# Counting edges per node: POOL makes the higher digit of four tiles in sixteen

## The chip, the cores and the metric

The kernel runs on one core of one Trainium2 chip. The metric is device time in microseconds for one launch, median of several runs. Engines: PE is TensorE, DVE is VectorE, ACT is ScalarE, POOL is GpSimd, SP is the queue that issues transfers.

## The reference, cut to what matters

```python
s, t = src, dst                       # 412500 edges, 12500 nodes
qe = (q[s] * scale) + edge_attr @ q_rpe_w + q_rpe_b
ke = k[t] + edge_attr @ k_rpe_w + k_rpe_b
ve = v[t] + edge_attr @ v_rpe_w + v_rpe_b
compat = einsum('ehd,ehd->eh', qe, ke)
attn = exp(compat - segment_max(compat, s)[s]) / segment_sum(...)
out = segment_sum(ve * attn, s)
return layernorm(x + out)
```

The edges are sorted by `dst`, and the softmax and the sums are over `s`. The kernel therefore needs, for each of the 12500 source nodes, how many edges it has (`deg`) and where its run of records begins (`base`). The change is in the counting of these edges alone.

## The kernel before, in words

There are three stages, one after the other: `tables_stage` (counts the edges of each node and makes the tables of q, k and v), `sort_stage` (writes one record per edge to its node's place in DRAM) and `attend_stage` (softmax and sums). The change is in `tables_stage`, which lasts to about 419 us.

A node number is split into a lower digit (7 bits, 128 values) and a higher digit (98 values, `NB`). The edges stand in 3232 tiles of 128, one edge to a partition. For one tile TensorE multiplies a one-hot matrix of the lower digits (128x128) by a one-hot matrix of the higher ones (128x98) and adds the product to `ps_hist` in PSUM, which counts edges by both digits. Tiles are taken in 202 groups of 16 (`GT`), with two sets of buffers (`NG`). For a group:

- VectorE makes `h_lo` for all 16 tiles in one instruction (L280, 2048 elements per partition) and `h_hi` for the first ten in another (L282, 980 elements). Each compares two operands that lie in SBUF: the table `value` and the digits.
- ScalarE makes the higher digit of the last six (`SIGNS`) as the sign of (digit - column + 0.5) over 99 columns, one instruction a tile (L388), with an input in PSUM. The product with `h_lo` is added to `ps_sign`. The difference of neighbouring columns is twice a one-hot, and it is halved at the end (L317, L318).
- TensorE (`tally`) waits for `one_rows`, does ten products (L344), waits for `hi_signs`, does six more (L348) and raises `tallied`. For the first 98 groups a product of the table of q, k, v (L361) follows each tally.

`tallied` starts at two, so that VectorE and ScalarE may make group g once group g-2 is tallied. After its first 12 groups VectorE works on the destination's windows and digits (L291 to L302) before it goes on. SP issues the transfers in a fixed order, and those of `xt` that TensorE's later products need stand behind ones that wait for this work. POOL sets a few constants (L229 to L239) and then does nothing until the next stage; there it issues the scatter of the records.

Only the later stages show POOL at arithmetic: in `attend_stage` it multiplies a part of the values by the probabilities (L1176), and makes a mask in two steps, `beyond` (L898, a subtraction of two operands) and `past` (L902, a comparison with zero, then a multiplication), with a semaphore between them. VectorE's large instructions there (L1176, L996) read one operand from SBUF and one from PSUM.

Of the kernel before, what the change touches and what calls it, by code (L numbers as in the profile page):

```python
# [8 lines left out]
BF16 = mybir.dt.bfloat16  # L9
I16 = mybir.dt.int16  # L10
I32 = mybir.dt.int32
ALU = mybir.AluOpType
# [3 lines left out]
P = 128  # L16
# [4 lines left out]
NB = math.ceil(N / P)  # L21
# [30 lines left out]
def gnn_kernel(nc, x, xT, src_lin, src_tiles, dst_lin, dst_tiles, attr, qkv_w, qkv_b, k_rpe_w, k_rpe_b,  # L52
# [9 lines left out]
    with ExitStack() as keep:  # L62
        def kept(name, shape, dt=F32):
            return keep.enter_context(nc.sbuf_tensor(name, shape, dt))

        T = dict(
            iota_row=kept("iota_row", [P, P], BF16),
            iota_f=kept("iota_f", [P, P]),
            iota_p=kept("iota_p", [P, 1]),
            ident=kept("ident", [P, P]),  # L70
            later=kept("later", [P, P]),
            q_tab=kept("q_tab", [P, NB, DH]),
            base=kept("base", [P, NB]),
            deg=kept("deg", [P, NB]),
            w_attr=kept("w_attr", [P, FEAT]),

            y=kept("y", [P, NB, DIM]),
            more=kept("more", [1, NB], I32),
            win_row=kept("win_row", [1, NCH], I32),
            flag=kept("flag", [1, 1], I32),  # L80
        )
        digits = keep.enter_context(ExitStack())
        T["lo_f"] = digits.enter_context(nc.sbuf_tensor("lo_f", [P, NT], F32))
        T["hi_f"] = digits.enter_context(nc.sbuf_tensor("hi_f", [P, NT], F32))
        T["src_f"] = digits.enter_context(nc.sbuf_tensor("src_f", [P, NT], F32))
        tables_stage(nc, T, xT, src_lin, src_tiles, dst_lin, qkv_w, qkv_b, k_rpe_w, k_rpe_b,
                     q_rpe_w, q_rpe_b, v_rpe_w, v_rpe_b, lo_dram, src_dram, dl_dram, win_dram, over_dram, kv_dram,
                     rec_dram)
        sort_stage(nc, T, x, attr, dst_tiles, lo_dram, src_dram, dl_dram, kv_dram, rec_dram)
        digits.close()  # L90
        attend_stage(nc, T, rec_dram, out)


def tables_stage(nc, T, xT, src_lin, src_tiles, dst_lin, qkv_w, qkv_b, k_rpe_w, k_rpe_b,
# [3 lines left out]

    iota_row, iota_f, iota_p, ident, later = (T[k] for k in ("iota_row", "iota_f", "iota_p", "ident", "later"))
    lo_f, hi_f, src_f, q_tab = (T[k] for k in ("lo_f", "hi_f", "src_f", "q_tab"))
    base, deg, w_attr = (T[k] for k in ("base", "deg", "w_attr"))
    win_row, flag = T["win_row"], T["flag"]
    GT, PAIRS, NG = 16, 8, 2
    SIGNS = 6
    HPAIRS = (GT - SIGNS) // 2
    GROUPS = NT // GT
    NXG = NB // XG
    with ExitStack() as ctx:  # L110
        def sb(name, shape, dt=F32):
            return ctx.enter_context(nc.sbuf_tensor(name, shape, dt))

        def sem(name):
            return ctx.enter_context(nc.semaphore(name))
# [6 lines left out]
        hi_w = sb("hi_w", [P, NT], BF16)  # L122
# [14 lines left out]
        h_lo = [sb(f"h_lo{i}", [P, PAIRS, P, 2], BF16) for i in range(NG)]  # L137
        h_hi = [sb(f"h_hi{i}", [P, HPAIRS, NB, 2], BF16) for i in range(NG)]
        s_hi = [sb(f"s_hi{i}", [P, SIGNS, NB + 1], BF16) for i in range(NG)]
        cols_half = sb("cols_half", [P, NB + 1])  # L140
        signs = sb("signs", [P, NB + 1])
        zeros = sb("zeros", [P, P], BF16)
# [5 lines left out]
        ps_sign = ctx.enter_context(nc.psum_tensor("ps_sign", [P, 512], F32))  # L148
# [6 lines left out]
        iotas, consts, diag = sem("iotas"), sem("consts"), sem("diag")  # L155
# [4 lines left out]
        narrowed, widened = sem("narrowed"), sem("widened")  # L160
        one_rows, tallied = sem("one_rows"), sem("tallied")
        half_made, half_copied, hi_signs = sem("half_made"), sem("half_copied"), sem("hi_signs")
        sums_made, rows_summed = sem("sums_made"), sem("rows_summed")
        tail_zero, tail_out = sem("tail_zero"), sem("tail_out")
        x_in = [sem(f"x_in{i}") for i in range(2)]
# [61 lines left out]
        @block.gpsimd  # L227
        def _(pool):
            pool.iota(iota_i[:, :], pattern=[[1, P]], base=0, channel_multiplier=0).then_inc(iotas, 1)  # L229
            pool.iota(iota_pi[:, :], pattern=[[0, 1]], base=0, channel_multiplier=1).then_inc(iotas, 1)  # L230
            pool.memset(ident[:, :], 0.0).then_inc(diag, 1)
            pool.memset(later[:, :], 1.0).then_inc(diag, 1)
            pool.wait_ge(diag, 2)
            pool.affine_select(out=ident[:, :], in_=ident[:, :], compare_op=ALU.not_equal, fill=1.0,
                               base=0, pattern=[[-1, P]], channel_multiplier=1).then_inc(diag, 1)

            pool.affine_select(out=later[:, :], in_=later[:, :], compare_op=ALU.is_gt, fill=0.0,
                               base=0, pattern=[[1, P]], channel_multiplier=-1).then_inc(diag, 1)
            pool.memset(tail[:, :], 0.0).then_inc(tail_zero, 1)  # L239
            pool.wait_ge(diag, 4)  # L240

        @block.vector
        def _(dve):
# [30 lines left out]
            def one_hots(g, i):  # L274

                def tiles(t, pairs, n):
                    return t[:, bass.ds(GT * g, 2 * pairs)].rearrange("p (k a t) -> p k a t", a=1, t=2).broadcast_to((P, pairs, n, 2))
# [3 lines left out]
                                  ALU.is_equal)  # L281
                dve.tensor_tensor(h_hi[i][:, :, :, :], value[:, 0:NB, :].unsqueeze(1).broadcast_to((P, HPAIRS, NB, 2)), tiles(hi_w, HPAIRS, NB),  # L282
                                  ALU.is_equal).then_inc(one_rows, 1)
# [49 lines left out]
        @block.tensor  # L333
        def _(pe):
            pe.sem_inc(tallied, NG)
            pe.wait_ge(consts, 5)
            for ps in (ps_hist, ps_sign):
                nc.tensor.matmul(ps[:, 0:NB + 1], zeros[:, :], zeros[:, 0:NB + 1], start=True, stop=False,
                                 skip_group_check=True)

            def tally(g, i):
                pe.wait_ge(one_rows, g + 1)
                for k in range(GT - SIGNS):
                    nc.tensor.matmul(ps_hist[:, 0:NB], h_lo[i][:, k // 2, :, k % 2], h_hi[i][:, k // 2, :, k % 2],  # L344
                                     start=False, stop=False, skip_group_check=True)
                pe.wait_ge(hi_signs, g + 1)
                for k in range(GT - SIGNS, GT):
                    last = nc.tensor.matmul(ps_sign[:, 0:NB + 1], h_lo[i][:, k // 2, :, k % 2], s_hi[i][:, k - (GT - SIGNS), :],  # L348
                                            start=False, stop=False, skip_group_check=True)
                last.then_inc(tallied, 1)  # L350

            pe.wait_ge(wq_in, 32)
            with pe.Fori(0, NXG // 2) as it:
                for i in range(2):
                    for b in range(XG):
                        tally(2 * XG * it + XG * i + b, (XG * i + b) % NG)
                        if b == 0:
                            pe.wait_ge(x_in[i], 16 * it + 16)

                            pe.wait_ge(q_read, 2 * it + i + 1)  # L360
                        last = nc.tensor.matmul(ps_x[i][:, b, :], xt[i][:, b * P:(b + 1) * P], w_qkv[:, :],  # L361
                                                start=True, stop=True)
                    last.then_inc(x_done, 1)
            with pe.Fori(NB // NG, GROUPS // NG) as it:
                for i in range(NG):
                    tally(NG * it + i, i)
            pe.wait_ge(sums_made, 1)
            pe.wait_ge(diag, 4)
            nc.tensor.matmul(ps_row[:, 0:1], later[:, :], incl[:, NB - 1:NB], start=True,
                             stop=True).then_inc(rows_summed, 1)  # L370

        @block.scalar
        def _(act):
# [11 lines left out]
            def higher(g, i):  # L385
                act.wait_ge(tallied, g + 1)
                for k in range(SIGNS):
                    last = act.activation(s_hi[i][:, k, :], ps_half[:, 0:NB + 1], ACT.Sign, scale=-1.0,  # L388
# [828 lines left out]
```

## Time and profile before

| what | value |
|---|---|
| three runs | 6689.97, 6712.76 (median), 6715.67 us |
| the profiled execution's own time | 6723.71 us |
| its span | 6722.0 us |
| stage of the change | to about 419 us of the span |
| DVE, ACT, PE, POOL busy over the span | 69%, 46%, 54%, 53% |

The profiled execution took 11 us more than the median of the runs. Shares of busy time are means over three stages with different limits, so the stage of the change is to be read by itself. In the rows below, durations of a single instruction are ns in groups by form, and us in timelines; a timeline row is start, duration, engine, line, operation, tiles, shape, and in brackets the engine's idle time before it. Instructions of one engine overlap a little, so the distance between two starts can be less than the first one's duration.

### The profile page before, as it was taken

What the parts mean: (1) busy time and instruction counts of PE and PEld (TensorE: products, weight loads), DVE (VectorE), ACT (ScalarE), POOL (GpSimd) and SP (SyncE); (2) the same over time, 40 slices, a digit from 0 to 9 for tenths busy, and PEclk for the clock granted to TensorE, in tenths of its full rate; (3) what the DMA queues carried; (4) which work ended last, traced back from release to release, by engine and by line L of the source; (5) the groups of instructions that cost most, each with busy time, mean ns of one, the idle gap of its engine ahead of it and who ended that gap; (6) DMA issues with size and microseconds to landing.
All of it is one profiled execution on the core that took longest, in us unless ns stands there. A gap on an engine that the chain in (4) does not pass through costs nothing. (4 is left out here: it accounts for less than half of the span.)

```text
span 6722.0 us, 113212 instructions
## 1 busy us (share of the span) xinstructions
PE 3642.7 (54%) x22344; PEld 3336.9 (50%) x22344; DVE 4669.1 (69%) x18275; ACT 3058.9 (46%) x7584; POOL 3596.2 (53%) x4030
## 2 busy tenths in 40 slices
PE   4654555545545555554555555545455554386786
PEld 3544445444445444444445454445454444365665
DVE  7986666666666666666666666666666666598998
ACT  5964444444444444444444444444444444322332
POOL 0025555555555555555555555555555555565664
PEclk8976665666666666666666666666666666698999
DMA  2013333333333333333333333333333333497897
GB/s 74 19 48 93 95 94 95 98 95 96 97 96 95 97 96 95 94 97 95 98 96 96 94 96 97 93 95 98 92 96 95 96 96 94 133 374 305 339 367 269
DMA packets 628039, 821.65 MB, mean 122 GB/s; under 512 B 216092, under 2 KB 561885, under 8 KB 615007
## 3 DMA queue, kind: packets, MB, share of 16 engines
q1 hardware_dynamic: 510185, 373.02, 21.9%
q0 software_dynamic: 117824, 448.32, 18.1%
q14 instruction: 22, 0.18, 0.0%
q8 instruction: 8, 0.13, 0.0%
HBM read 644.87 MB, written 176.01 MB: 122 GB/s over the span
## 5 line engine op out<-in xcount | busy, mean ns | idle before, releaser
L542 POOL DMA_INDIRECT rec_dram<-recs,place_i x3232 | 3093.7, 957 | 2751.9 <-DVE recs L596 1828.1
L630 PE MATMUL ps_cnt<-hi_hot,lo_hot 128*128 128x98 bf16 x3232 | 371.1, 259 | 2563.8 <-ACT free_rec L691 1615.5
L674 ACT ACTIVATE lo_hotT<-lo_b,minus_p 128x512 f32<-128x512 bf16 x808 | 582.9, 721 | 2585.8 <-DMA w_in<-kv_dram 2300.2
L573 DVE SCALAR_TENSOR_TENSOR matches<-src_b,src_f,ps_const 128x128 bf16<-128x128 int16 (+3 forms) x3232 | 1582.3, 543 | 67.7 <-issue 52.5
L630 PEld LDWEIGHTS ps_cnt<-hi_hot,lo_hot 128*128 128x128 bf16 x3232 | 239.0, 120 | 2730.4 <-issue 2420.5
L639 PE MATMUL ps_look<-free_rec,lo_hotT 128*128 128x98 f32 x6464 | 1408.2, 389 | 2.9 <-ACT lo_hotT L680 2.9
L656 PE MATMUL ps_feat<-w_in,edge_in 115*128 115x128 f32 x6464 | 1348.3, 375 | 44.8 <-issue 44.5
L582 DVE CUSTOM_DVE_ANT_0 picked<-hi_hot,ps_look 128x98 f32<-128x98 bf16 x3232 | 642.3, 252 | 1015.2 <-remote 803.0
L639 PEld LDWEIGHTS ps_look<-free_rec,lo_hotT 128*128 128x128 f32 x6464 | 1286.1, 294 | 3.1 <-ACT lo_hotT L680 3.1
L656 PEld LDWEIGHTS ps_feat<-w_in,edge_in 115*128 115x128 f32 x6464 | 1247.9, 286 | 43.6 <-issue 43.4
L962 PE MATMUL ps_sum<-msg,ident 128*128 128x256 f32 x2744 | 624.5, 386 | 237.7 <-DVE msg L1176 237.7
L596 DVE TENSOR_REDUCE recs<-qk 128x16 f32<-128x128 f32 x808 | 231.3, 286 | 661.5 <-remote 537.4
L962 PEld LDWEIGHTS ps_sum<-msg,ident 128*128 128x128 f32 x2744 | 518.6, 192 | 343.3 <-DVE msg L1176 275.2
L680 ACT ACTIVATE lo_hotT<-lo_hotT,one 128x512 f32<-128x512 f32 x808 | 573.3, 710 | 0.0
L683 ACT ACTIVATE edge_in<-edge_in,one 96x512 f32<-96x512 f32 x808 | 573.1, 709 | 0.0
L676 ACT ACTIVATE edge_in<-dst_b,minus_p 96x512 f32<-96x512 bf16 x808 | 570.0, 705 | 0.0
L564 DVE TENSOR_TENSOR lo_hot<-lo_f,ps_const 128x512 bf16<-128x512 bf16 (+1 forms) x808 | 551.7, 683 | 12.6 <-issue 12.6
L566 DVE TENSOR_TENSOR hi_hot<-hi_f,ps_const 128x392 bf16<-128x392 bf16 (+1 forms) x808 | 449.2, 556 | 8.1 <-issue 7.8
L667 ACT ACTIVATE recs<-ps_feat 128x384 f32<-128x384 f32 x808 | 379.9, 470 | 2.8 <-DMA rec_dram<-recs,place_i 1.7
L1121 ACT ACTIVATE ps_prob<-ps_lg,neg 128x56 f32<-128x56 f32 x392 | 109.3, 279 | 536.1 <-DVE neg L1011 536.1
L388 ACT ACTIVATE s_hi<-ps_half,hi_f 128x99 bf16<-128x99 f32 x1212 | 303.5, 366 | 77.7 <-PE ps_sign L348 77.4
L691 ACT ACTIVATE free_rec<-ps_cnt 128x98 f32<-128x98 f32 x808 | 188.3, 233 | 330.7 <-remote 305.5
(152 smaller groups left out, 3419.1 us busy)
## 6 DMA issues: line engine op xcount, KB each, us to landing
lo_b<-lo_dram SPq DMA_DIRECT2D x808, 128.0 KB
src_b<-src_dram SPq DMA_DIRECT2D x808, 128.0 KB
dst_b<-dl_dram SPq DMA_DIRECT2D x808, 96.0 KB
rec_dram<-recs,place_i POOLq DMA_INDIRECT x3232
edge_in<-in_attr SPq DMA_DIRECT2D x808, 36.0 KB
w_in<-kv_dram SPq DMA_DIRECT2D x808, 36.0 KB
kv_dram<-kvt SPq DMA_DIRECT2D x14, 336.0 KB, 2.7
xt<-in_xT SPq DMA_DIRECT2D x14, 224.0 KB, 3.3
```

What stands on the lines that cost most here:

```text
L542: pool.indirect_dma_start(rec_dram[:, :], bass.IndirectOffsetOnAxis(place_i[j][:, m:m + 1], 0), recs[j][:, m, :], None).then_inc(scattered ...
L564: dve.tensor_tensor(lo_hot[j][:, :, :], lo_f[:, tiles].unsqueeze(2).broadcast_to((P, CT, P)), ps_const[:, 0:1, :].broadcast_to((P, CT, P)) ...
L573: last = dve.scalar_tensor_tensor(matches[j][:, m, 0:before], src_b[j][:, 0:before], src_f[:, bass.ds(u * CT + m, 1)], ps_const[:, CT - m: ...
L582: ins = dve.tensor_tensor_reduce(out=picked[j][:, m, :], in0=hi_hot[j][:, m, :], in1=ps_look[j % 2][:, m, 0:NB], scale=1.0, scalar=0.0, op ...
L630: last = nc.tensor.matmul(ps_cnt[:, 0:NB], lo_hot[j][:, m, :], hi_hot[j][:, m, :], start=False, stop=False, skip_group_check=True)
L639: last = nc.tensor.matmul(ps_look[j % 2][:, m, 0:NB], lo_hotT[j][:, P * m:P * (m + 1)], free_rec[j % 2][:, :], start=True, stop=True)
L656: last = nc.tensor.matmul(ps_feat[j][:, m, :], edge_in[j][0:K_ROWS, tile], w_in[j][0:K_ROWS, :], start=True, stop=True)
L674: act.activation(lo_hotT[j][:, :], lo_b[j][:, :], ACT.Abs, bias=minus_p[:, 0:1]).then_inc(lo_off, 1)
L676: act.activation(edge_in[j][0:WIN, :], dst_b[j][:, :], ACT.Abs, bias=minus_p[0:WIN, 0:1]).then_inc(dst_off, 1)
L680: act.activation(lo_hotT[j][:, :], lo_hotT[j][:, :], ACT.Relu, scale=-1.0, bias=one[:, 0:1]).then_inc(lo_hotT_made, 1)
L683: act.activation(edge_in[j][0:WIN, :], edge_in[j][0:WIN, :], ACT.Relu, scale=-1.0, bias=one[0:WIN, 0:1]).then_inc(dst_hotT_made, 1)
L962: last = nc.tensor.matmul(ps_sum[i][:, 0:SUM, :], ident[:, :], msg[i][:, k:k + SUM, :], start=(k == 0), stop=(k + SUM == S0))
```

## The change

The first ten tiles of a group are divided anew. VectorE makes one-hots of the higher digit for six (`HPAIRS` goes from 5 to 3). For the next four (`STEPS`) POOL makes steps: it subtracts the column number from the digit (`fall`, 4x99 elements per partition, two operands in SBUF, bf16), waits for that, and turns the difference into 2 where it is at least zero and 0 elsewhere (`t_hi`). The difference of neighbouring columns of such a step is twice a one-hot, as with the signs, so TensorE adds the products with these tiles to `ps_sign`. It waits for `hi_steps` before them. POOL waits for `tallied` like the other two.

```diff
--- before.py
+++ after.py
@@ -98,13 +98,14 @@
 
 
 
+
     iota_row, iota_f, iota_p, ident, later = (T[k] for k in ("iota_row", "iota_f", "iota_p", "ident", "later"))
     lo_f, hi_f, src_f, q_tab = (T[k] for k in ("lo_f", "hi_f", "src_f", "q_tab"))
     base, deg, w_attr = (T[k] for k in ("base", "deg", "w_attr"))
     win_row, flag = T["win_row"], T["flag"]
     GT, PAIRS, NG = 16, 8, 2
-    SIGNS = 6
-    HPAIRS = (GT - SIGNS) // 2
+    SIGNS, STEPS = 6, 4
+    HPAIRS = (GT - SIGNS - STEPS) // 2
     GROUPS = NT // GT
     NXG = NB // XG
     with ExitStack() as ctx:
@@ -137,6 +138,8 @@
         h_lo = [sb(f"h_lo{i}", [P, PAIRS, P, 2], BF16) for i in range(NG)]
         h_hi = [sb(f"h_hi{i}", [P, HPAIRS, NB, 2], BF16) for i in range(NG)]
         s_hi = [sb(f"s_hi{i}", [P, SIGNS, NB + 1], BF16) for i in range(NG)]
+        t_hi = [sb(f"t_hi{i}", [P, STEPS, NB + 1], BF16) for i in range(NG)]
+        fall = [sb(f"fall{i}", [P, STEPS, NB + 1], BF16) for i in range(NG)]
         cols_half = sb("cols_half", [P, NB + 1])
         signs = sb("signs", [P, NB + 1])
         zeros = sb("zeros", [P, P], BF16)
@@ -160,6 +163,7 @@
         narrowed, widened = sem("narrowed"), sem("widened")
         one_rows, tallied = sem("one_rows"), sem("tallied")
         half_made, half_copied, hi_signs = sem("half_made"), sem("half_copied"), sem("hi_signs")
+        hi_falls, hi_steps, pool_groups = sem("hi_falls"), sem("hi_steps"), sem("pool_groups")
         sums_made, rows_summed = sem("sums_made"), sem("rows_summed")
         tail_zero, tail_out = sem("tail_zero"), sem("tail_out")
         x_in = [sem(f"x_in{i}") for i in range(2)]
@@ -238,6 +242,22 @@
                                base=0, pattern=[[1, P]], channel_multiplier=-1).then_inc(diag, 1)
             pool.memset(tail[:, :], 0.0).then_inc(tail_zero, 1)
             pool.wait_ge(diag, 4)
+            pool.wait_ge(consts, 5)
+            pool.wait_ge(narrowed, 2)
+
+            def higher(g, i):
+
+                pool.wait_ge(tallied, g + 1)
+                pool.sem_inc(pool_groups, 1)
+                pool.tensor_tensor(fall[i][:, :, :], hi_w[:, bass.ds(GT * g + 2 * HPAIRS, STEPS)].unsqueeze(2).broadcast_to((P, STEPS, NB + 1)),
+                                   iota_row[:, 0:NB + 1].unsqueeze(1).broadcast_to((P, STEPS, NB + 1)), ALU.subtract).then_inc(hi_falls, 1)
+                pool.wait_ge(hi_falls, g + 1)
+                pool.sem_inc(pool_groups, 1)
+                pool.tensor_scalar(t_hi[i][:, :, :], fall[i][:, :, :], 0.0, 2.0, ALU.is_ge, ALU.mult).then_inc(hi_steps, 1)
+
+            with pool.Fori(0, GROUPS // NG) as it:
+                for i in range(NG):
+                    higher(NG * it + i, i)
 
         @block.vector
         def _(dve):
@@ -340,8 +360,12 @@
 
             def tally(g, i):
                 pe.wait_ge(one_rows, g + 1)
-                for k in range(GT - SIGNS):
+                for k in range(2 * HPAIRS):
                     nc.tensor.matmul(ps_hist[:, 0:NB], h_lo[i][:, k // 2, :, k % 2], h_hi[i][:, k // 2, :, k % 2],
+                                     start=False, stop=False, skip_group_check=True)
+                pe.wait_ge(hi_steps, g + 1)
+                for k in range(STEPS):
+                    nc.tensor.matmul(ps_sign[:, 0:NB + 1], h_lo[i][:, HPAIRS + k // 2, :, k % 2], t_hi[i][:, k, :],
                                      start=False, stop=False, skip_group_check=True)
                 pe.wait_ge(hi_signs, g + 1)
                 for k in range(GT - SIGNS, GT):
```

## Rows read from the trace of the kernel before

**Rows 1.** The page of the profile: busy share in 40 slices

```profile
DVE  7986666666666666666666666666666666598998
```

**Rows 2.** Busy time by stretch (x is instructions; then clock, DMA)

```profile
300.00:400.00 100.00, 53.43 (x930) 44.65 (x931) 100.00 (x118) 88.17 (x352) 0.00 (x0) 1.00 0.00 0
```

**Rows 3.** Groups of instructions by form, 80 to 400 us

```profile
L388 ACT ACTIVATE s_hi<-ps_half,hi_f 128x99 bf16<-128x99 f32 x1066 | 267.2, 365 | 56.0 <-PE ps_sign L348 55.8
L280 DVE TENSOR_TENSOR h_lo<-value,lo_w 128x2048 bf16<-128x2048 bf16 x178 | 216.1, 1214 | 27.7 <-PE ps_sign L348 27.6
L282 DVE TENSOR_TENSOR h_hi<-value,hi_w 128x980 bf16<-128x980 bf16 x177 | 116.6, 659 | 0.0
```

**Rows 4.** The timeline of one beat, 299 to 304 us

```profile
300.35 1.21 DVE L280 TENSOR_TENSOR h_lo<-value,lo_w 128x2048 bf16<-128x2048 bf16 x1
...
300.49 0.64 PE L344 MATMUL ps_hist<-h_hi,h_lo 128*128 128x98 bf16 x10 [0.79 <-DVE h_hi L282]
...
301.56 1.51 ACT L388 ACTIVATE s_hi<-ps_half,hi_f 128x99 bf16<-128x99 f32 x6 [0.21 <-PE ps_sign L348]
302.06 1.21 DVE L280 TENSOR_TENSOR h_lo<-value,lo_w 128x2048 bf16<-128x2048 bf16 x1
```

**Rows 5.** POOL's instructions by form, whole span

```profile
L1176 POOL TENSOR_TENSOR msg<-rec,prob_s 128x1024 f32<-128x1024 f32 x98 | 198.0, 2021 | 47.1 <-ACT prob_s L1132 47.1
...
L905 POOL TENSOR_TENSOR known<-rec,past 128x224 f32<-128x224 f32 x98 | 58.0, 592 | 41.0 <-DMA rec<-rec_dram,idx 34.5 <-POOL past L902 4.9
L902 POOL TENSOR_SCALAR past<-beyond 128x56 f32<-128x56 f32 x98 | 40.4, 412 | 19.3 <-POOL beyond L898 19.3
...
L898 POOL TENSOR_TENSOR beyond<-iota_f,deg 128x56 f32<-128x56 f32 x98 | 27.4, 280 | 0.0
L887 POOL COPY idx<-start_i 128x1 int32 x92 | 16.7, 181 | 44.2 <-DVE msg L1176 43.7
...
L234 POOL TENSOR_SCALAR_AFFINE_SELECT ident<-ident 128x128 f32<-128x128 f32 x1 | 0.3, 293 | 0.2 <-POOL later L232 0.2
```

**Rows 6.** The timeline, 6201 to 6219 us: VectorE and POOL together

```profile
6199.51 2.02 POOL L1176 TENSOR_TENSOR msg<-rec,prob_s 128x1024 f32<-128x1024 f32 x1 [0.45 <-ACT prob_s L1132]
6200.11 1.45 DVE L1049 TENSOR_SCALAR past_x<-iota_f,left 128x16 f32<-128x16 f32 x1
...
6201.48 0.29 POOL L898 TENSOR_TENSOR beyond<-iota_f,deg 128x56 f32<-128x56 f32 x1
6201.60 0.15 DVE L1050 TENSOR_SCALAR next_x<-next_x  x1
...
6201.97 0.41 POOL L902 TENSOR_SCALAR past<-beyond 128x56 f32<-128x56 f32 x1 [0.20 <-POOL beyond L898]
```

**Rows 7.** Line 1176: count, then duration in ns, least, median, most

```profile
L1176 DVE TENSOR_TENSOR msg<-rec,ps_prob x196: 1454/1478/1489, 5879.5 to 6684.9; 128x1280 f32<-128x1280 f32 x196
L1176 POOL TENSOR_TENSOR msg<-rec,prob_s x98: 2009/2021/2030, 5878.2 to 6683.5; 128x1024 f32<-128x1024 f32 x98
```

**Rows 8.** The timeline, 6000 to 6025 us: two large products side by side

```profile
6004.60 2.02 POOL L1176 TENSOR_TENSOR msg<-rec,prob_s 128x1024 f32<-128x1024 f32 x1 [0.37 <-ACT prob_s L1132]
...
6004.95 1.48 DVE L1176 TENSOR_TENSOR msg<-rec,ps_prob 128x1280 f32<-128x1280 f32 x1
```

**Rows 9.** The timeline, first 46 us: VectorE waits, and turns to the windows

```profile
24.22 1.23 DVE L280 TENSOR_TENSOR h_lo<-value,lo_w 128x2048 bf16<-128x2048 bf16 x1 [2.98 <-PE ps_sign L348]
...
41.70 4.41 DVE L291 TENSOR_REDUCE win_f<-dst_l 101x8 f32<-101x4096 int32 x1
```

**Rows 10.** The timeline, 59 to 100 us: VectorE comes back; a stall

```profile
59.51 1.22 DVE L280 TENSOR_TENSOR h_lo<-value,lo_w 128x2048 bf16<-128x2048 bf16 x1
...
61.37 1.00 PE L344 MATMUL ps_hist<-h_hi,h_lo 128*128 128x98 bf16 x10 [18.32 <-DVE h_hi L282]
...
93.73 0.79 PE L361 MATMUL ps_x<-w_qkv,xt 65*128 65x128 f32 x2 [27.48 <-DMA xt<-in_xT]
...
95.99 1.22 DVE L280 TENSOR_TENSOR h_lo<-value,lo_w 128x2048 bf16<-128x2048 bf16 x1 [27.58 <-PE ps_sign L348]
```

## The prediction

> **What bounds the kernel now.** I read the page first, for where the changed stage lies: VectorE is busy for 70 and 90% of the first two slices of 40, 168 us each, and for 60% or so in the long stage behind them [rows 1]. Then the busy time by stretch: between 300 and 400 us VectorE is busy for 100.00 us of 100, ScalarE for 88, TensorE for 53, POOL for 0, at the full clock (2.4 GHz) [rows 2]. So here VectorE sets the pace, ScalarE is close behind, and POOL is free. Then the groups by form, for the price of each part [rows 3], and the timeline, for the beat: one group begins at 300.35 us and the next at 302.06, so a group costs 1.71 us, though the durations add up to 1.214 + 0.659 = 1.87 [rows 3, 4]; an instruction starts before the one ahead has ended. ScalarE's six signs take 1.51 us and then it waits 0.21 for the tally, and TensorE waits 0.79 us for h_hi before each tally [rows 4]. The 202 groups cost 202 x 1.71 = 345 us. This stage comes before the others and none of it overlaps them, so what a group gains or loses is multiplied by 202 and reaches the end.
>
> **VectorE: what goes.** h_lo stays whole. h_hi shrinks from 980 to 588 elements. The two forms differ by 2048 - 980 = 1068 elements and 1214 - 659 = 555 ns, that is 0.52 ns an element [rows 3]; 392 elements fewer save 0.20 us. VectorE's own beat becomes 1.71 - 0.20 = 1.51 us. If nothing else were late, ScalarE at 1.51 us would be level with it and the stage would win 202 x 0.20 = 40 us. That is the most that the change can bring.
>
> **POOL: what is added.** Each group gets two instructions of 4 x 99 = 396 elements, the second waiting for the first.
> - The subtraction has two inputs in SBUF. POOL's such forms: 56 elements 280 ns, 224 elements 592, 1024 elements 2021 [rows 5]. The last two give 1429 / 800 = 1.79 ns an element, the first two 1.86. So 592 + 172 x 1.79 = 900 ns. These rows are float32; the new form is bf16, with one operand spread over 99 columns, which no row has. I take 0.90 us, with 0.80 to 1.10 as bounds.
> - Between two dependent instructions POOL sits idle for 0.20 us, as at 6201.97 us [rows 6].
> - The comparison and multiplication has one row, 56 elements for 412 ns [rows 5]. Its price per element is bounded below by the one-input rows, 1 element 181 ns and 128 elements 293 (0.88 ns an element), and above by the two-input slope. So 412 + 340 x 0.88 = 711 ns, or 412 + 340 x 1.79 = 1020 ns. I take the middle, 0.87 us: one input speaks for the low end, two operations for the high one.
>
> Alone, POOL needs 0.90 + 0.20 + 0.87 = 1.97 us for a group (bounds 1.71 to 2.32). That is more than the 1.71 us of now. Two sets of buffers don't help a stage whose throughput is too low: POOL becomes the pace even undisturbed.
>
> **Do the two engines disturb each other?** The trace has a place that shows that they can. At 6200.11 us VectorE starts an instruction on 16 elements, while POOL's multiplication runs from 6199.51 to 6201.53; VectorE's ends at 6201.56, after 1.45 us, and right behind it an instruction of the same kind on one element takes 0.15 us [rows 6]. The small one waited for POOL's to end, 0.03 us before. Not every pair does that: the one-element instruction ran beside POOL's `beyond` [rows 6], and VectorE's large products, of which one starts at 6004.95 us inside POOL's of 6004.60, take 1454 to 1489 ns in all 196 cases and POOL's 2009 to 2030 [rows 7, 8]. Those have one operand in PSUM, as the names ps_prob say. The new pairs are of neither kind: h_lo and h_hi read both operands from SBUF, and so does POOL's subtraction. No row has such a pair, so the price of standing together lies between nothing and the whole of both. I take the whole: the row that was blocked has all its operands in SBUF on both sides, as the new pairs have, and the large rows that were not blocked differ from them just by the PSUM operand. Then the instructions of the two engines take turns. POOL's 0.20 us of idling is covered by VectorE's turn, and a group costs 1.51 + 0.90 + 0.87 = 3.28 us. For its own range: 1.51 + 0.80 + 0.71 = 3.02 at the low end; if VectorE's instructions no longer start before the one ahead has ended, 1.87 - 0.20 + 1.10 + 1.02 = 3.79 at the high one.
>
> On this the Trainium skill has a rule (SBUF — State Buffer, section "Who interferes with whom"): a VectorE instruction with two SBUF inputs and a GpSimd instruction that reads SBUF share a read interface, whoever is first holds it for the whole instruction, and the other blocks; with at most one SBUF input and outside the two-port modes there is no conflict. The blocked row at 6200.11 and the undisturbed L1176 rows agree with it, but the rule's case for two SBUF inputs is shown by no row here. By the rule a group would cost what the turns above cost; with it wrong for tensor_tensor, the 1.97 us of POOL alone.
>
> **What is taken off again.** (a) At 24.22 us VectorE has waited 2.98 us for ScalarE's first signs [rows 9]; a slower start covers those 3 us. (b) From 41.70 to 59.51 us VectorE works on the windows [rows 9, 10], and in that time the steps of the two groups ahead are made with no VectorE instruction of the count beside them: 2 x 1.77 = 3.5 us. (c) After it TensorE stands 27.48 us for xt, which lands 34 us after VectorE came back [rows 10]; SP issues it behind transfers that wait for VectorE's window work, so it moves with that and not with the groups. The three groups tallied in those 34 us can each be 1.57 us slower for nothing: 5 us. Together 12 us.
>
> **What hangs on the new wait.** TensorE waits for `hi_steps` in the middle of a tally. Behind it stand four step products, six sign products and, in the first 98 groups, the product for the tables, for which ScalarE and then SP wait; all of them have a beat to spare. With TensorE idle for most of the beat its clock may fall to 1.2 GHz, where ten products take 1.00 us [rows 10] in place of 0.64 [rows 4]. The ten that follow POOL are late by that, but VectorE and POOL still have the other buffer's group before them, which takes longer. I cost it at nothing; without that cover it is 0.4 us a group. POOL's start is no cost: the digits that it waits for are those that VectorE's first h_hi needs. After its last group POOL goes on to the next stage, where it has nothing to send until later.
>
> **The sum.** 202 x (3.28 - 1.71) = 317 us, less 12, is +305 us. Against the profiled execution's own 6723.7 us that is 7029; this execution was 11 us over the median of the runs, so the median should come to about 7018. I say 7020. The range of this case: 202 x (3.02 - 1.71) - 12 = +253 to 202 x (3.79 - 1.71) - 12 = +408, that is 6965 to 7120.
>
> **The rivals.**
> - *No blocking, POOL is the pace.* For it: the large products keep their time side by side, and a one-element instruction too [rows 6 to 8]. Against: the blocked one [rows 6]. The price is 202 x (1.97 - 1.71) = +53 us; (a) and (c) take off 3 + 1 us, so 6713 + 49 = 6762. With POOL at its bounds, 1.71 to 2.32 us, it is 6709 to 6832.
> - *POOL is quick enough, and the change gains.* The other side: the one mechanism is that POOL's pair costs less than 1.71 us, with no blocking. For it only the low bounds above, both at once, and a smaller price for bf16, which no row shows. At 1.51 us ScalarE and VectorE set the pace: 6713 - 40 = 6673. It decides at 1.71 us for the pair.
> - *Blocking only for one of POOL's two instructions.* The second reads one operand in place of two; were it free of the turns, a group would cost VectorE's 1.51 plus the 0.90 us, 2.41 us, which also holds the pair with its wait: 202 x 0.70 - 8 = +133, 6846.
> - That the change doesn't do what it says can be ruled out: digit minus column is at least zero up to the digit's own column, so neighbouring columns of the steps differ by 2 there and by 0 elsewhere, which is what halving after the sums needs.
>
> **How the numbers follow.** Turns for both instructions 0.65, for one of them 0.08, no blocking with POOL as the pace 0.20, a gain or a draw 0.07. The predicted time is that of the first, 7020. The range has to take in most of the second and third, and the first one's bounds: 6735 to 7130, which leaves out the gain, the lower part of the third case and a little above. A measurement of this kernel can tell about 0.5%, 34 us, from no change. Of the third case about a fifth lies within that, and of the last about half gains more. So: faster 0.03, same 0.08, slower 0.89.
>
> **What would show it.** Right: VectorE and POOL alternate in the timeline between 100 and 700 us, the beat is 3.0 to 3.8 us, durations of h_lo or of POOL's pair are stretched over their price when they meet, h_hi alone is 0.45 us, and the count ends near 725 us in place of 419. The stages after it last as long as before. Wrong: h_lo at 1.21 us right beside a POOL instruction in progress (then the beat is POOL's 1.8 to 2.3 us); or POOL idle in each beat with TensorE waiting for ScalarE, which would be the gain.

## The result, and the profile after

The changed kernel takes 6994.05 us (median of 4 runs, 6980.8 to 7016.14) against 6711.2 us (4 runs) before: ratio 1.0431, 95% interval 1.0396 to 1.0466. It is 283 us slower (4.3%). The forecast was 7020 us.

The stage of the count is where the time went. Its first step after the counting is a copy of the sums to `signs`; here it is before and after, in the timelines (start, duration):

```profile
416.43 0.26 DVE L316 COPY signs<-ps_sign 128x99 f32<-128x99 f32 x1 [1.59 <-PE ps_sign L348]
```

```profile
701.00 0.26 DVE L336 COPY signs<-ps_sign 128x99 f32<-128x99 f32 x1 [4.37 <-PE ps_sign L372]
```

The count ends 284.6 us later. The spans of the two profiled executions differ by 269 us, so the later stages account for no loss.

The busy time by stretch of the changed kernel (PE, PEld, DVE, ACT, POOL, granted clock, share of transfers, GB/s), to be read against [rows 2]:

```profile
300.00:400.00 100.00, 59.71 (x549) 51.69 (x550) 57.02 (x63) 50.29 (x194) 93.95 (x64) 0.50 0.07 18
```

POOL is busy for 94 us of 100 and VectorE for 57 in place of 100. The granted clock is 0.50, TensorE's lower level of 1.2 GHz, where it was 1.00 before. The waits name the same pace (120 to 600 us; total, times, longest):

```profile
ACT s_hi L412 <- PE ps_sign L372: 242.8, 150, 2.3
...
PE ps_sign L368 <- POOL t_hi L256: 209.7, 150, 2.3
DVE h_lo L300 <- PE ps_sign L372: 204.4, 151, 1.9
```

In each group everyone waits for POOL's second instruction: TensorE directly, ScalarE and VectorE by way of the tally. POOL itself waits for nobody in this stretch; its only idle time is the 0.20 us between its two instructions. The groups by form, beside [rows 3]:

```profile
L256 POOL TENSOR_SCALAR t_hi<-fall 128x396 bf16<-128x396 bf16 x151 | 306.2, 2028 | 29.5 <-POOL fall L252 29.5
...
L300 DVE TENSOR_TENSOR h_lo<-value,lo_w 128x2048 bf16<-128x2048 bf16 x151 | 197.5, 1308 | 204.4 <-PE ps_sign L372 204.4
L252 POOL TENSOR_TENSOR fall<-hi_w,iota_row 128x396 bf16<-128x396 bf16 x150 | 150.7, 1005 | 0.0
...
L302 DVE TENSOR_TENSOR h_hi<-value,hi_w 128x588 bf16<-128x588 bf16 x151 | 92.7, 614 | 0.0
```

The means hide two kinds of group. The timeline, beside [rows 4], shows a pattern that repeats every two groups (TensorE left out but for one row):

```profile
639.82 0.85 POOL L252 TENSOR_TENSOR fall<-hi_w,iota_row 128x396 bf16<-128x396 bf16 x1
...
640.87 1.54 POOL L256 TENSOR_SCALAR t_hi<-fall 128x396 bf16<-128x396 bf16 x1 [0.20 <-POOL fall L252]
641.07 1.39 DVE L300 TENSOR_TENSOR h_lo<-value,lo_w 128x2048 bf16<-128x2048 bf16 x1 [1.93 <-PE ps_sign L372]
...
642.38 1.16 POOL L252 TENSOR_TENSOR fall<-hi_w,iota_row 128x396 bf16<-128x396 bf16 x1
642.38 0.45 DVE L302 TENSOR_TENSOR h_hi<-value,hi_w 128x588 bf16<-128x588 bf16 x1
...
642.46 0.52 PE L368 MATMUL ps_sign<-t_hi,h_lo 128*128 128x99 bf16 x4 [1.05 <-POOL t_hi L256]
...
643.62 1.23 DVE L300 TENSOR_TENSOR h_lo<-value,lo_w 128x2048 bf16<-128x2048 bf16 x1 [0.79 <-PE ps_sign L372]
...
643.74 2.51 POOL L256 TENSOR_SCALAR t_hi<-fall 128x396 bf16<-128x396 bf16 x1 [0.20 <-POOL fall L252]
644.77 0.77 DVE L302 TENSOR_TENSOR h_hi<-value,hi_w 128x588 bf16<-128x588 bf16 x1
646.22 0.85 POOL L252 TENSOR_TENSOR fall<-hi_w,iota_row 128x396 bf16<-128x396 bf16 x1
...
647.26 1.54 POOL L256 TENSOR_SCALAR t_hi<-fall 128x396 bf16<-128x396 bf16 x1 [0.20 <-POOL fall L252]
```

From 639.82 to 646.22 us two groups are made: 6.40 us, so a group costs 3.20 us where the forecast had 3.28. In the first, the comparison begins 0.20 us ahead of h_lo and takes 1.54 us; h_lo takes 1.39 in place of 1.21. In the second, h_lo begins 0.12 us ahead and the comparison takes 2.51 us. The subtraction takes 0.85 us by itself and 1.16 when h_hi starts with it.

### The profile page after: what moved, and what is told of

It is laid out like the page before. It is cut to its first block and busy times, and to the rows that moved or that the text cites. A ratio compares the mean times of both kernels' runs of the same rounds, so it can differ in the third digit from the quotient of the medians.

```text
span 6991.0 us, 114627 instructions
## 1 busy us (share of the span) xinstructions
PE 3741.4 (54%) x22344; PEld 3424.0 (49%) x22344; DVE 4693.4 (67%) x18275; ACT 3059.9 (44%) x7584; POOL 4203.3 (60%) x4434
## 5 line engine op out<-in xcount | busy, mean ns | idle before, releaser
L663 PE MATMUL ps_look<-free_rec,lo_hotT 128*128 128x98 f32 x6464 | 1386.5, 384 | 2.7 <-ACT lo_hotT L704 2.7
L680 PE MATMUL ps_feat<-w_in,edge_in 115*128 115x128 f32 x6464 | 1333.5, 372 | 46.7 <-issue 46.4
L663 PEld LDWEIGHTS ps_look<-free_rec,lo_hotT 128*128 128x128 f32 x6464 | 1265.8, 290 | 2.9 <-ACT lo_hotT L704 2.9
L300 DVE TENSOR_TENSOR h_lo<-value,lo_w 128x2048 bf16<-128x2048 bf16 x202 | 265.1, 1312 | 286.2 <-PE ps_sign L372 286.2
L256 POOL TENSOR_SCALAR t_hi<-fall 128x396 bf16<-128x396 bf16 x202 | 405.5, 2007 | 39.4 <-POOL fall L252 39.4
```

Source lines behind the costliest of these rows:

```text
L663: last = nc.tensor.matmul(ps_look[j % 2][:, m, 0:NB], lo_hotT[j][:, P * m:P * (m + 1)], free_rec[j % 2][:, :], start=True, stop=True)
L680: last = nc.tensor.matmul(ps_feat[j][:, m, :], edge_in[j][0:K_ROWS, tile], w_in[j][0:K_ROWS, :], start=True, stop=True)
```

## The experiments

In the expectations F is POOL's first instruction, the subtraction, and T its second, the comparison with its multiplication. A beat is the time from one group to the next. A hold is the time for which one engine keeps the other waiting.

**First set.** Here the kernel before took 6724.72 us (7 runs). Two of the four kernels (the first and the second) are the count's stage alone, with wrong counts; only where their count ends is of use. The time of the third is that of one run. The first takes POOL's reading away.

```diff
-                pool.tensor_tensor(fall[i][:, :, :], hi_w[...], iota_row[...], ALU.subtract).then_inc(hi_falls, 1)
-                pool.wait_ge(hi_falls, g + 1)
-                pool.tensor_scalar(t_hi[i][:, :, :], fall[i][:, :, :], 0.0, 2.0, ALU.is_ge, ALU.mult).then_inc(hi_steps, 1)
+                pool.memset(t_hi[i][:, :, :], 2.0).then_inc(hi_steps, 1)
```

> The stage of the count alone (the two later stages are left out, and POOL's two instructions are replaced by one that only fills t_hi with a constant, so the counts are not counts). Theory: POOL's own price (1.54 us for the comparison, 0.85 us for the subtraction) and the waits of the two engines for each other's SBUF operands are all of the loss, and the rest of the change is a gain. Then a group costs 1.51 to 1.55 us, ScalarE and VectorE set the pace, and the stage ends near 419 - 202 x 0.18 = 383 us. Rival: the split of the tally, with its wait in the middle and its slow-clock products, costs by itself: a group stays over 1.71 us and the stage ends at 419 us or later.

The timeline of this kernel near 300 us:

```profile
299.69 0.43 POOL L264 MEMSET t_hi<- 128x396 bf16 x1 [1.09 <-PE ps_sign L380]
300.00 1.21 DVE L308 TENSOR_TENSOR h_lo<-value,lo_w 128x2048 bf16<-128x2048 bf16 x1
...
301.13 0.45 DVE L310 TENSOR_TENSOR h_hi<-value,hi_w 128x588 bf16<-128x588 bf16 x1
301.20 0.43 POOL L264 MEMSET t_hi<- 128x396 bf16 x1 [1.08 <-PE ps_sign L380]
301.51 1.21 DVE L308 TENSOR_TENSOR h_lo<-value,lo_w 128x2048 bf16<-128x2048 bf16 x1
```

A beat is 1.51 us, h_lo takes 1.21 and h_hi 0.45 us with POOL's instruction beside them, and the copy to `signs` comes at 377.8 us, 38.6 us earlier than before. The split of the tally costs nothing here, and a POOL instruction that only writes disturbs nobody. The rest of the change is worth what the forecast had as its most, 40 us. One thing differs from the changed kernel besides POOL's reading: TensorE's granted clock was 1.00 between 200 and 300 us, against 0.50 there.

The second takes VectorE away: its one-hots are filled once ahead, and a fill of 96 elements (0.10 us) stands for them in the loop.

```diff
-                dve.tensor_tensor(h_lo[i][:, :, :, :], value[...], tiles(lo_w, PAIRS, P), ALU.is_equal)
-                dve.tensor_tensor(h_hi[i][:, :, :, :], value[...], tiles(hi_w, HPAIRS, NB), ALU.is_equal).then_inc(one_rows, 1)
+                dve.memset(h_hi[i][:, :, 0:16, :], 0.0).then_inc(one_rows, 1)
```

> The stage of the count alone, with VectorE's h_lo and h_hi made once ahead and only a 96-element fill in their place in the loop (two later stages and the true counts left out). Theory: POOL is the pace even undisturbed: F 0.85 us, 0.20 idle, T 1.54 us, a group every 2.56 us, and the wait for VectorE's reads goes from 0.64 us a group to nothing; no T of 2.51 us, no F of 1.16 us. The stage ends near 17 + 202 x 2.56 + 13 for the windows + about 20 for the transfer = 567 us. Rival: the 1.54 us of T are themselves waiting for VectorE, and POOL alone takes about 0.9 + 0.2 + 0.9 = 2.0 us a group: the stage ends near 450 us.

Its POOL instructions over all 202 groups (count, then duration in ns, least, median, most):

```profile
L264 POOL TENSOR_TENSOR fall<-hi_w,iota_row x202: 848/851/2047, 17.7 to 572.2; 128x396 bf16<-128x396 bf16 x101
L268 POOL TENSOR_SCALAR t_hi<-fall x202: 1538/1540/1547, 19.9 to 573.2; 128x396 bf16<-128x396 bf16 x101
```

A comparison never takes more than 1547 ns and never less than 1538: this is POOL's price and no wait. A group costs 2.56 us (comparisons begin at 299.64 and 302.20 us), and the copy comes at 575.9 us (567 expected), 159.5 us later than before. VectorE's part, put back, brings it to 701.0: another 125 us, or 0.62 us a group.

The third puts POOL's loop of the changed kernel (its function `higher` with both instructions) into the kernel before; VectorE, ScalarE and TensorE stay as they were, and none of them waits for it.

```diff
+            with pool.Fori(0, GROUPS // NG) as it:
+                for i in range(NG):
+                    higher(NG * it + i, i)
```

> The kernel before, whole and with right results, with POOL's two instructions run beside VectorE's full ones; nobody waits for them within the count, though the stage can't close before POOL is through. Asked: by how much VectorE's beat of 1.71 us grows. Theory of reads: POOL holds VectorE off only while it reads, about 0.65 us for the subtraction and 0.3 us for the comparison, in each of its own groups of 3 to 4 us: VectorE's beat is 2.1 to 2.3 us, and h_lo shows durations between 1.2 and 1.9 us. Theory of whole turns (the forecast's): VectorE's h_lo and h_hi and POOL's two take turns, the beat is about 1.71 + 0.85 + 1.54 = 4.1 us. Third: only POOL is held off, the beat stays 1.71 us.

Seven microseconds of it, VectorE and POOL:

```profile
297.93 1.73 POOL L256 TENSOR_SCALAR t_hi<-fall 128x396 bf16<-128x396 bf16 x1 [0.20 <-POOL fall L252]
298.18 1.53 DVE L300 TENSOR_TENSOR h_lo<-value,lo_w 128x2048 bf16<-128x2048 bf16 x1
...
299.63 1.36 POOL L252 TENSOR_TENSOR fall<-hi_w,iota_row 128x396 bf16<-128x396 bf16 x1
299.63 0.65 DVE L302 TENSOR_TENSOR h_hi<-value,hi_w 128x980 bf16<-128x980 bf16 x1
...
300.21 1.86 DVE L300 TENSOR_TENSOR h_lo<-value,lo_w 128x2048 bf16<-128x2048 bf16 x1
...
301.19 2.28 POOL L256 TENSOR_SCALAR t_hi<-fall 128x396 bf16<-128x396 bf16 x1 [0.20 <-POOL fall L252]
...
302.00 0.97 DVE L302 TENSOR_TENSOR h_hi<-value,hi_w 128x980 bf16<-128x980 bf16 x1
302.89 1.21 DVE L300 TENSOR_TENSOR h_lo<-value,lo_w 128x2048 bf16<-128x2048 bf16 x1
...
303.45 1.36 POOL L252 TENSOR_TENSOR fall<-hi_w,iota_row 128x396 bf16<-128x396 bf16 x1
...
304.03 1.31 DVE L302 TENSOR_TENSOR h_hi<-value,hi_w 128x980 bf16<-128x980 bf16 x1
...
305.26 1.53 DVE L300 TENSOR_TENSOR h_lo<-value,lo_w 128x2048 bf16<-128x2048 bf16 x1
```

From 298.18 to 305.26 us VectorE makes three groups, 2.36 us each, and POOL makes two (comparisons at 297.93 and 301.19, subtractions at 299.63 and 303.45). The amounts by which VectorE's instructions are stretched come in two sizes. A comparison of POOL's costs 0.32 us: h_lo 1.53 in place of 1.21, h_hi 0.97 in place of 0.65. A subtraction costs 0.65 us: h_lo 1.86, h_hi 1.31. Two of each in three groups are 1.94 / 3 = 0.65 us, and 1.71 + 0.65 is the beat of 2.36. Neither whole turns (4.1 us) nor an undisturbed VectorE (1.71 us) is left; the theory of reads holds, a little above its 2.1 to 2.3. Over the whole count the copy to `signs` comes at 543.9 us, 127.5 us later than before, or 0.63 us a group. The total of 6991.76 us means only that the stage can't close before POOL is through.

The fourth drops the second operation of the comparison.

```diff
-                pool.tensor_scalar(t_hi[i][:, :, :], fall[i][:, :, :], 0.0, 2.0, ALU.is_ge, ALU.mult).then_inc(hi_steps, 1)
+                pool.tensor_scalar(t_hi[i][:, :, :], fall[i][:, :, :], 0.0, None, ALU.is_ge).then_inc(hi_steps, 1)
-                    nc.tensor.matmul(ps_sign[:, 0:NB + 1], h_lo[...], t_hi[i][:, k, :], ...)
+                    nc.tensor.matmul(ps_sign[:, P:P + NB + 1], h_lo[...], t_hi[i][:, k, :], ...)
+            step(dve.scalar_tensor_tensor(signs[:, :], ps_sign[:, P:P + NB + 1], 2.0, signs[:, :], ALU.mult, ALU.add))
```

> The change, with right results, where POOL's second instruction compares but does not multiply (steps of 1, summed in columns of their own and doubled at the end, one instruction more on VectorE there). Theory A, the second operation is what made T cost 1.54 us: T falls to about 1.0 us, a group from 3.20 to 2.7 us, and the kernel takes about 6890 us. Theory B, the price is that of bf16 or of the elements and not of the second operation: T stays at 1.4 to 1.55 us and the kernel at 6980 to 7000 us.

```profile
298.67 1.13 POOL L252 TENSOR_TENSOR fall<-hi_w,iota_row 128x396 bf16<-128x396 bf16 x1
...
299.02 1.10 DVE L302 TENSOR_TENSOR h_hi<-value,hi_w 128x588 bf16<-128x588 bf16 x1
...
299.99 1.20 POOL L256 TENSOR_SCALAR t_hi<-fall 128x396 bf16<-128x396 bf16 x1 [0.20 <-POOL fall L252]
300.04 1.54 DVE L300 TENSOR_TENSOR h_lo<-value,lo_w 128x2048 bf16<-128x2048 bf16 x1
...
301.16 1.14 POOL L252 TENSOR_TENSOR fall<-hi_w,iota_row 128x396 bf16<-128x396 bf16 x1
...
301.51 1.11 DVE L302 TENSOR_TENSOR h_hi<-value,hi_w 128x588 bf16<-128x588 bf16 x1
...
302.49 1.20 POOL L256 TENSOR_SCALAR t_hi<-fall 128x396 bf16<-128x396 bf16 x1 [0.20 <-POOL fall L252]
```

6859.03 us, ratio to before 1.0203 (1.0177 to 1.0230). The comparison takes 1.20 us, so the second operation costs 0.34 us, not the 0.5 that theory A had; but the count ends at 567.4 us, 133.6 earlier than in the changed kernel, more than theory A's 100. The beat falls from 3.20 to 2.49 us, by twice what POOL saves, and the order in which the engines meet is another: POOL's comparison now begins just ahead of h_lo, group after group, and is not stretched (1197 ns at the least and in the median of all 202). That this order is what the rest of the gain comes from is read from the timeline, not tested by itself. Here VectorE is busy for 100.00 us of 100 and sets the pace: 1.51 us of its own, 0.33 for the comparison (h_lo 1.54) and 0.65 for the subtraction (h_hi 1.11) are 2.49.

**Second set.** This chip ran the kernel before in 5405.76 us (11 runs), so only differences are read; the count itself ends where it did (700.7 us in the second kernel below, against 701.0). The first makes steps for two tiles.

```diff
-    SIGNS, STEPS = 6, 4
+    SIGNS, STEPS = 6, 2
```

> The change for two tiles in sixteen in place of four (VectorE makes eight; right results). Theory of holds, from the runs so far: POOL keeps VectorE off while it reads, 0.65 us for the subtraction and 0.33 us for the comparison of four tiles, so about half for two; VectorE's beat is 1.61 + 0.33 + 0.17 = 2.1 us, VectorE is busy 100%, and POOL's pair alone (0.50 + 0.20 + about 0.9 = 1.6 us) is not the pace. Kernel: 6720 + 202 x 0.4 - 10 = 6790 us. Rival, POOL's price alone: the pair at 1.6 us is under 1.71 us, so the change gains, 6700 us. Rival, whole turns: 1.61 + 0.5 + 0.9 = 3.0 us, 6970 us.

5478.4 us (4 runs), 72.6 more than before (70 expected), ratio 1.0135 (1.0121 to 1.0150). The beat is 2.08 us (h_lo starts at 299.15 and 301.23 us): 1.61 us of VectorE's own, 0.15 us held by the comparison (h_lo 1.36 us) and 0.32 by the subtraction (h_hi 0.88), half of those for four tiles.

The second changes the type of the difference.

```diff
-        fall = [sb(f"fall{i}", [P, STEPS, NB + 1], BF16) for i in range(NG)]
+        fall = [sb(f"fall{i}", [P, STEPS, NB + 1]) for i in range(NG)]
```

> The change with the difference between POOL's two instructions in float32 (right results). Asked: is it bf16 that made the comparison cost 1.54 us where the float32 row of the kernel before gave 0.7 to 1.0? Theory A, no: price by element and operation; T undisturbed stays at 1.5 us and the kernel at about 6990 us. Theory B, the narrow type is slow to read: T undisturbed falls to about 1.0 us and the kernel to about 6880 us. A float32 operand is twice the bytes, so T may also hold VectorE for longer than 0.33 us.

5684.88 us (one run), 279 more than before, as with bf16 (283). The comparison takes 1537 ns at the least and 1538 in the median. The type is not it: theory A. Its price by size: 56 elements 412 ns [rows 5], 198 elements 892 ns (the least in the version for two tiles), 396 elements 1540 ns, so 3.3 ns an element with two operations.

The third and fourth have no subtraction. For four tiles, and then for two:

```diff
-                pool.tensor_tensor(fall[i][:, :, :], ...)
-                pool.tensor_scalar(t_hi[i][:, :, :], fall[i][:, :, :], 0.0, 2.0, ALU.is_ge, ALU.mult).then_inc(hi_steps, 1)
+                for k in range(STEPS):
+                    last = pool.tensor_scalar(t_hi[i][:, k, :], iota_row[:, 0:NB + 1], hi_f[:, tile:tile + 1], 2.0, ALU.is_le, ALU.mult)
+                last.then_inc(hi_steps, 1)
```

> The change for four tiles with no subtraction: one instruction a tile compares the 99 columns with the digit of each partition and doubles, so POOL reads one operand and not two (right results; POOL's loop is written out). Theory of holds: no hold of 0.65 us; four short ones, together 0.33 to 0.5 us, so VectorE could keep 1.51 + 0.4 = 1.9 us; POOL needs 4 x 0.55 = 2.2 us by the two rows of 56 and 396 elements (412 and 1540 ns), plus what it waits for VectorE, so POOL is the pace at 2.3 to 2.9 us: 6830 to 6940 us. Rival: what counts is how many instructions POOL starts while VectorE reads, each waiting for the end of VectorE's; then four a group cost more than two, 3.2 us or more, 7000 us.

> As the version with one instruction a tile, for two tiles (VectorE makes eight of the ten; right results). POOL's 2 x 0.55 = 1.1 us are far from the pace, so this is the gentlest form. Theory of holds: VectorE is let off 0.10 us a group and held for 0.17 to 0.3 us, since POOL's reading (0.33 us for 396 elements, 0.83 ns each) costs VectorE more than VectorE's own work on the element (0.52 ns): beat 1.68 to 1.85 us, the kernel 0 to 30 us slower than before, no gain. Rival: the holds vanish where POOL reads little at a time; beat 1.61 us, 20 us faster than before.

Groups by form of the two-tile version (120 to 360 us), of POOL and of VectorE:

```profile
L253 POOL TENSOR_SCALAR t_hi<-iota_row,hi_f 128x99 bf16<-128x99 bf16 x196 | 242.7, 1260 | 0.0
```

```profile
L298 DVE TENSOR_TENSOR h_lo<-value,lo_w 128x2048 bf16<-128x2048 bf16 x98 | 121.1, 1236 | 76.0 <-PE ps_sign L370 75.9
L300 DVE TENSOR_TENSOR h_hi<-value,hi_w 128x784 bf16<-128x784 bf16 x97 | 54.1, 558 | 0.0
```

Both expectations by holds failed, and on the same side. Four tiles: 5743.52 us, +338, ratio 1.0626 (1.0611 to 1.0642), worse than the change. Two tiles: 5547.86 us, +142, ratio 1.0263 (1.0249 to 1.0276), worse than with the pair, and outside the rival's too, which had a gain. VectorE is hardly held (h_lo 1236 ns, h_hi 558), but POOL is, and it became the pace: it is busy for 100.00 us of 100. The mean of 1260 ns hides two kinds again. Here are two instructions of POOL's in a row in the two-tile version:

```profile
300.85 0.64 POOL L253 TENSOR_SCALAR t_hi<-iota_row,hi_f 128x99 bf16<-128x99 bf16 x1
301.46 1.97 POOL L253 TENSOR_SCALAR t_hi<-iota_row,hi_f 128x99 bf16<-128x99 bf16 x1
```

The first meets no instruction of VectorE's. The second starts 0.15 us behind an h_lo (301.31 us) and lasts past the h_hi behind it (302.45 to 303.01 us), 1.33 us longer than its price. Of 404 instructions 198 are of this kind. With four tiles it is one in four (198 of 808 take over 1.5 us, and the median is 638 ns). So the rival for four tiles came near in time (it had 7000 us, +280 over its base), but not each instruction waits: one a group does.

**Last run.** VectorE's table goes to PSUM, for h_lo as shown and for h_hi alike. This kernel and the one before ran once each here.

```diff
+            step(dve.tensor_copy(ps_row[:, P:3 * P], value[:, :, :].rearrange("p n t -> p (n t)")))
+            value_p = ps_row[:, P:3 * P].rearrange("p (n t) -> p n t", t=2)
-                dve.tensor_tensor(h_lo[i][:, :, :, :], value[:, :, :]..., tiles(lo_w, PAIRS, P), ALU.is_equal)
+                dve.tensor_tensor(h_lo[i][:, :, :, :], value_p..., tiles(lo_w, PAIRS, P), ALU.is_equal)
```

> The change, with right results, where the table of digit values that VectorE compares with lies in PSUM, in float32, so h_lo and h_hi read one operand from SBUF and not two. VectorE's own work gets slower: about 1.2 to 1.3 ns an element by the row lo_hot of the kernel before (512 elements 683 ns), so h_lo 2.2 to 2.6 us and h_hi 0.7 to 0.8 us. Theory, the hold is for the second SBUF operand: POOL's pair is undisturbed in every group (the subtraction 0.85 us, the comparison 1.54 us, none of 1.16 or 2.51) and VectorE's h_lo and h_hi have one duration each (spread under 0.05 us); the beat is VectorE's own 2.9 to 3.3 us. Rival, any two instructions of the two engines that use SBUF wait for each other: durations spread by 0.3 to 1 us as in the changed kernel, and the beat is 3.5 us or more.

```profile
L302 DVE TENSOR_TENSOR h_lo<-ps_row,lo_w x202: 2268/2271/2292, 17.7 to 637.6; 128x2048 bf16<-128x2048 f32 x101
```

```profile
L304 DVE TENSOR_TENSOR h_hi<-ps_row,hi_w x202: 748/749/760, 19.9 to 639.8; 128x588 bf16<-128x588 f32 x101
```

```profile
L252 POOL TENSOR_TENSOR fall<-hi_w,iota_row x202: 848/848/2036, 16.5 to 635.3; 128x396 bf16<-128x396 bf16 x101
L256 POOL TENSOR_SCALAR t_hi<-fall x202: 1537/1538/1544, 18.7 to 636.4; 128x396 bf16<-128x396 bf16 x101
```

All four have one duration (the one subtraction of 2036 ns is the first, beside a cast of VectorE's), though both engines work at once: in 200 to 300 us VectorE is busy for 100.00 us and POOL for 82.93. The beat is VectorE's 2.88 us, and the kernel takes 5624.46 us against 5401.35, 223 more. So it is not enough that both engines use SBUF: with one operand of VectorE's in PSUM, neither holds the other off. The edit changes more than the operand's place, though. The table is float32, and h_lo takes 1.11 ns an element where the write-only version has 0.59. No run has a float32 table in SBUF, so that the place alone does it is likely and not shown.

## Why the prediction was right, and where its sum was not

*VectorE's part.* h_hi at 0.45 us and a beat of 1.51 us without POOL's reading: as forecast, shown by the write-only version.

*The subtraction.* 0.85 us against 0.90 forecast.

*The comparison.* 1.54 us against 0.87, beyond the bound of 1.02. The step of the sum that failed is the price per element, bounded by two inputs at 1.79 ns: a comparison and a multiplication of one input cost 3.3 ns an element. The middle was taken between bounds of which neither came from an instruction with two operations. The one row of the same form had a single size, and so no slope.

*Whole turns.* The forecast let VectorE's 1.51 us and POOL's pair exclude each other. In fact POOL holds VectorE off for 0.65 us of its subtraction's 0.85, but only for 0.33 us of its comparison's 1.54; and VectorE, if it reads first, holds POOL off to its end. Per two groups POOL loses 0.97 us at a comparison and 0.31 at a subtraction, 0.64 a group, where the forecast charged 1.51. So a group is 0.85 + 0.20 + 1.54 - 0.03 + 0.64 = 3.20 us against 0.90 + 0.87 + 1.51 = 3.28. Off by +0.67 for the comparison, -0.87 for the turns, +0.17 for an idle gap that nothing covers and -0.05 for the subtraction, the terms meet in nearly the same sum. The total was right by more luck than its steps deserve; that POOL becomes the pace, that both engines hold each other off, and the sign, were right for their reasons.

On the turns, the Trainium skill (SBUF — State Buffer, section "Who interferes with whom") has a VectorE instruction with two SBUF inputs against a GpSimd instruction that reads SBUF as a case that conflicts, and at most one SBUF input, or a GpSimd instruction that only writes, as cases that don't. The last run and the write-only one agree (h_lo 2268 to 2292 ns, 1203 to 1227 ns). It calls the shared ports an exclusive lock, and has whoever issues first keep them for the whole instruction; that sentence stands with VectorE's two-port modes, and the forecast carried it over to these reads. VectorE's h_lo does so here, but a comparison of 1.54 us kept h_lo off for 0.33 us.

*What was taken off.* 202 x (3.20 - 1.71) = 301 us, and the count ended 284.6 later: 16 us taken off, 12 forecast. TensorE's lower clock kept nobody waiting by itself: at 642.46 us the products of the steps start 0.05 us after the comparison ends (640.87 + 1.54), so none of the six products before them was in the way, and from 120 to 600 us POOL never waits for the tally. But h_lo starts when the tally ends, 1.16 us after those products begin, and by 0.12 or 0.20 us that decides which engine reads first. Products at the upper clock would end the tally sooner; no run has the changed kernel so, and what order and what beat would follow is open.

*The rivals.* POOL's price without any blocking (+49 us) fell short on both counts: alone it costs 159.5 us, and the blocking 125. The gain exists, 38.6 us, but only if POOL doesn't read. Blocking for one of POOL's instructions (6846 us) fell short as well: VectorE loses twice as much to the subtraction as to the comparison, but both count.

The mechanism is shown by opposite edits (VectorE taken away, POOL's reading taken away, one operand moved). That POOL's comparison reads ahead and lets go, which would explain 0.33 us, is inferred from the stretches and not shown. They fit it well: an h_lo that starts 0.05 us behind the comparison loses 0.33 us, with two operations (1.54 us long, at 109.91 us of the changed kernel) as with one (1.20 us long), and one that starts 0.20 us behind loses 0.18. So each hold ends 0.38 us after the comparison's start, however long the comparison lasts. Why a 99-element instruction that meets h_lo waits for most of the h_hi behind it too (0.64 us becomes 1.97), when the comparison of 396 elements gets in between the two (1.54 becomes 2.51), is open. So is the small instruction of the later stage that waited for POOL's product [rows 6]: no run took it apart.

## What to carry to other kernels

Before work is moved from VectorE to POOL, count what POOL's reading takes from VectorE: here 0.33 us for 396 elements of one operand, 0.83 ns an element, and 0.65 us for the subtraction's two, against 0.52 ns that VectorE spends on an element itself. In this kernel, where VectorE sets the pace and reads two operands from SBUF, no split that was tried gained, whether by two tiles or four, one operation or two, or one instruction a tile. And an engine's price per element has to come from two sizes of the same form with as many operations; a slope borrowed from another form was off by nearly two here.

## What the runs showed of the hardware that was not expected

- An instruction's duration in the profile includes its wait for the other engine: POOL's comparison is 1537 ns or 2513 ns, VectorE's h_hi 450 to 1115 ns.
- Who starts first decides who pays, and it decides much: with h_lo 0.12 us ahead POOL's comparison waited 0.97 us, while with h_lo 0.20 us behind VectorE lost 0.18 us.
- A POOL fill of 396 bf16 elements (427 ns) beside VectorE leaves h_lo at 1203 to 1227 ns.
- The view of the clock can mislead. It gives 1.00 for the version with the PSUM operand between 200 and 300 us. But that trace has its first record of the clock at 660 us, and the view shows 1.00 where there is none. The products there go at the pace of the lower level. In the changed kernel six products take 0.69 us at a granted clock of 0.50, and 0.45 us in the one short stretch of the count with a record of 1.00 (76.04 to 79.45 us). Here are that stretch, the lower level, and last the version with the PSUM operand:

```profile
76.94 0.45 PE L364 MATMUL ps_hist<-h_hi,h_lo 128*128 128x98 bf16 x6 [0.38 <-DVE h_hi L302]
640.72 0.69 PE L364 MATMUL ps_hist<-h_hi,h_lo 128*128 128x98 bf16 x6
...
300.07 0.67 PE L366 MATMUL ps_hist<-h_hi,h_lo 128*128 128x98 bf16 x6 [0.81 <-DVE h_hi L304]
```
